# Attention kernel on one Trainium2 core: how the queries reach their stacked layout

## The reference

```python
qh = q.reshape(B, S, 16, 16); kh = k.reshape(B, S, 16, 16)
q1 = einsum('bshd,hed->bshe', qh, wq1); k1 = einsum('bshd,hed->bshe', kh, wk1)   # and q2, k2
s1 = einsum('bshe,bthe->bhst', q1, k1) / 4                                        # and s2
attn = softmax(s1) - gain * softmax(s2)
o = einsum('bhst,bthe->bshe', attn, vp)     # then normed per head, times wo, added to x
```

## Time and profile before

| | |
|---|---|
| median of 3 runs | 1498.9 us (1498.68 to 1508.15) |
| profiled execution | 1502.58 us, its span 1500.8 us |
| first attention | about 27 to 770 us of the span |
| PE busy in the span | 1335.3 us (89%), granted clock 0.963 on average |
| DVE, ACT, POOL busy | 1182.6, 1076.6, 729.9 us |

### The profile page before, as it was taken

How to read it: one execution, slowest core, us unless ns; L and a number is a source line. 1 busy time by engine, 2 the same in 40 slices (tenths; PEclk the granted TensorE clock), 3 DMA queues, 4 the chain that set the end, 5 groups by cost and what they waited for, 6 DMA issues and landing times. The chain is left out here.

```text
span 1500.8 us, 30949 instructions
## 1 busy us (share of the span) xinstructions
PE 1335.3 (89%) x11612; PEld 904.7 (60%) x11612; DVE 1182.6 (79%) x1964; ACT 1076.6 (72%) x1810; POOL 729.9 (49%) x1154
## 2 busy tenths in 40 slices
PE   4799999999999999999978999996899986377686
PEld 3566666666666666666645666665667665133374
DVE  4478888788788788877768999985547999799775
ACT  2377777777777777777747888886455655699996
POOL 2156766757676576676665333421126667521000
PEclk9999999999999999999979999999899889599899
DMA  8655866866676685675310000000544442187399
GB/s 165 114 102 102 154 103 116 140 108 130 114 136 114 123 135 99 111 129 99 89 30 1 1 1 1 1 1 19 185 129 116 128 117 65 39 333 305 130 403 365
DMA packets 126469, 178.31 MB, mean 119 GB/s; under 512 B 47586, under 2 KB 78434, under 8 KB 120162
## 3 DMA queue, kind: packets, MB, share of 16 engines
q1 hardware_dynamic: 126032, 176.32, 49.6%
q10 hardware_dynamic: 288, 0.00, 0.0%
HBM read 82.36 MB, written 41.94 MB: 83 GB/s over the span
## 5 line engine op out<-in xcount | busy, mean ns | idle before, releaser
L735 DVE TENSOR_REDUCE neg_max<-psum 128x8 f32<-128x1024 f32 x256 | 313.2, 1223 | 70.4 <-PE psum L544 65.7
L672 ACT ACTIVATE exp_t<-psum 128x512 f32<-128x512 f32 x512 | 281.6, 597 | 49.3 <-PE psum L557 49.1
L838 POOL TENSOR_TENSOR rs<-rs,minus_half 128x16 f32<-128x16 f32 x64 | 186.3, 2912 | 5.0
L557 PEld LDWEIGHTS psum<-q_stack,k_stack 50*128 50x128 f32 x2048 | 137.5, 192 | 78.5 <-issue 75.2
L557 PE MATMUL psum<-q_stack,k_stack 50*128 50x128 f32 x2048 | 173.6, 290 | 0.8 <-ACT exp_t L672 0.8
L568 PE MATMUL psum<-exp_t,v_pad 128*32 128x256 f32 x2048 | 167.6, 400 | 0.0
L677 ACT ACTIVATE o_t<-psum 128x512 f32<-128x512 f32 x128 | 76.5, 598 | 95.6 <-PE psum L568 95.3
L544 PE MATMUL psum<-k_stack,q_stack 48*128 48x256 f32 x1024 | 136.1, 345 | 6.9 <-DVE neg_max L735 6.4
L943 PE MATMUL psum<-f_w,f_xqt 128*128 128x512 bf16 x512 | 125.1, 387 | 5.1 <-DVE f_hid L1071 5.0
L830 POOL TENSOR_TENSOR sq<-u 128x256 f32<-128x256 f32 x64 | 39.2, 612 | 175.7 <-DVE u L752 174.8
L544 PEld LDWEIGHTS psum<-k_stack,q_stack 48*128 48x128 f32 x1024 | 82.6, 193 | 55.8 <-issue 44.3
(11 more groups left out here) (220 smaller groups left out, 3050.4 us busy)
## 6 DMA issues: line engine op xcount, KB each, us to landing
k_stack<-k_hi SPq DMA_DIRECT2D x256, 128.0 KB, 4.6
g_scratch<-f_gelu SPq DMA_DIRECT2D x24, 1024.0 KB, 3.9
f_gelu<-g_scratch SPq DMA_DIRECT2D x24, 1024.0 KB, 14.9
k_stack<-k_lo SPq DMA_DIRECT2D x128, 128.0 KB, 4.7
ctx_t<-in_ctx_t SPq DMA_DIRECT2D x32, 256.0 KB, 5.3
x_state<-in_x SPq DMA_DIRECT2D x16, 512.0 KB, 6.6
v_in<-in_ctx SPq DMA_DIRECT2D x32, 256.0 KB, 5.7
v_scratch<-v_in SPq DMA_DIRECT2D x32, 256.0 KB, 5.0
```

The lines of the kernel that those rows point to most:

```text
L557: r = e.matmul(psum[:, 2 + j, o:o + P], self.k_st[rows, b // 2 % self.NK, pair // 2 % 2, pair % 2, i, pair // 4, b % 2, :], self.q_st[rows ...
L672: e.activation(self.prob[:, n % 3, j].rearrange("p n w t -> p (n w t)"), psum[:, 2 + j, :], ACT.Exp).then_inc(s["exp"], 1)
L735: e.tensor_reduce(self.negm[:, b % 2, :, :, 2 * u:2 * u + 2].rearrange("p j w n -> p j n w"), psum[:, 0:2, :].rearrange("p j (n w k) -> p ...
L838: e.tensor_tensor(self.rs[:, i], self.rs[:, i], self.expo[:, :], ALU.pow).then_inc(s["pool"], 1)
```

## The change

Queries now go the keys' way, in pairs. POOL writes `xn` of both sequences of a pair, its channels reordered within each half. PE turns them as they are, four transposes for the pair (`turn_queries(p)`, tick 16p-14). ACT copies the high part out of PSUM (`q_high`), DVE the rest (`rest_queries`), and SP stacks them by six transfers of 128 KB into 16 partitions each (`stack_queries(p)`, tick 16p-10). `maxima` waits for them to land. The copies into `q_stack` and the spread buffer are gone. `q_stack` has three slots of a pair instead of four of a sequence, `k_hi` and `k_lo` one buffer instead of two. POOL norms queries two sequences further ahead, so x is loaded two sequences earlier, except the second group of eight, which follows the first queries' transfers. Heads are paired differently, and `wo_t` and the index into `v_pad` are permuted to match. A buffer of the next stage moves, with a wait for the end of the attention.

```diff
-    NQ, NK, NC = 4, KEY_SLOTS, 2
+    NQ, NK, NC = 3, KEY_SLOTS, 2
...
+        def stack_queries(p):
+            k = p % self.NQ
+            w.wait_ge(s["q_lo"], p + 1)
+            w.wait_ge(s["st_pe"], 8 * (p - self.NQ + 1))
+            for j in range(2):
+                for part, src in ((0, self.q_hi), (1, self.q_hi), (2, self.q_lo)):
+                    row = SLOT * j + HD0 * part
+                    e.dma_start(self.q_st[row:row + HD0, k].rearrange("e n h s q -> e n (h s q)").bitcast(F32),
+                                src[SLOT * j:SLOT * j + SLOT].rearrange("p h s q -> p (h s q)").bitcast(F32)
+                                ).then_inc(s["q_st"], 16)
...
+            if u == 6 and b % 2 == 0 and 0 <= b + 2 < NSEQ:
+                stack_queries((b + 2) // 2)
             if u == 6 and b in self.CENTRE_LOAD:
...
-            if u == 7 and b % 8 in (2, 4) and 0 <= b // 8 < 6:
-                load_x(b // 8 + 2, b % 8 // 2 - 1)
-            if tick == -12:
+            if u == 7 and b % 8 in (0, 2) and 0 <= b // 8 < 6:
+                load_x(b // 8 + 2, b % 8 // 2)
+            if tick == -8:
...
-        def turn_queries(b, half):
-            w.wait_ge(s["q_lo"], b + 1)
+        def turn_queries(p):
+            w.wait_ge(s["q_norm"], 2 * p + 2)
             w.wait_ge(sh.s["const_loaded"], 16)
...
+            w.wait_ge(s["k_lo"], 2 * p + 2)
+            for h in range(2):
+                for i in range(2):
+                    r = e.transpose(psum[:, 7, (2 * h + i) * P:(2 * h + i + 1) * P],
+                                    self.xn[:, i, h * P:(h + 1) * P], ident[:, :])
             r.then_inc(s["q_t"], 1)
 
         def maxima(b, u):
             n = 4 * b + u
-            w.wait_ge(s["q_st"], 2 * b + 2)
+            self.q_landed(w, b // 2)
...
-                if u in (2, 4) and 0 <= b + 1 < NSEQ:
-                    turn_queries(b + 1, u // 2 - 1)
+                if u == 2 and b % 2 == 0 and 0 <= b + 2 < NSEQ:
+                    turn_queries((b + 2) // 2)
...
-            if p >= 2:
-                self.k_landed(w, p - 2)
+            if p:
+                self.k_landed(w, p - 1)
...
+        def q_high(p):
+            w.wait_ge(s["q_t"], p + 1)
+            if p:
+                self.q_landed(w, p - 1)
+            e.activation(self.q_hi[:, :, :, :].rearrange("p h s q -> p (h s q)"), psum[:, 7, :], ACT.Copy).then_inc(s["q_hi"], 1)
...
-        def q_stack(b, half):
...
+        def rest_queries(p):
+            flat = lambda z: z[:, :, :, :].rearrange("p h s q -> p (h s q)")
+            w.wait_ge(s["q_hi"], p + 1)
+            e.tensor_tensor(flat(self.q_lo), psum[:, 7, :], flat(self.q_hi).bitcast(F32), ALU.subtract).then_inc(s["q_lo"], 1)
...
-            w.wait_ge(s["q_lo"], b - 1)
-            w.wait_ge(s["q_hi"], b - 1)
-            sh.normed(e, self.xn[:, b % 2], b).then_inc(s["q_norm"], 1)
+            w.wait_ge(s["q_t"], b // 2)
...
-            if 0 <= b + 2 < NSEQ:
-                normed_queries(b + 2)
+            if 0 <= b + 4 < NSEQ:
+                normed_queries(b + 4)
...
+            a0.late_free(w)
```

More of the change, by code:

```diff
@@ L332, in __init__ @@
         self.ctx_t = sb("ctx_t", [P, self.NC, 2, 2, P])
[L333 to L335 removed]
+        self.k_hi = sb("k_hi", [P, 2, 2, 2, P], F32R)
+        self.k_lo = sb("k_lo", [P, 2, 2, 2, P], F32R)
+        self.q_hi = sb("q_hi", [P, 2, 2, P], F32R)
+        self.q_lo = sb("q_lo", [P, 2, 2, P], F32R)
         self.xn = sb("xn", [P, 2, D])
[L338 removed]
+        self.q_st = sb("q_stack", [P, self.NQ, 4, 2, 2, P], F32R)
         self.v_pad = sb("v_pad", [P, 2, 2, NH0, VPAD])
@@ L537, in maxima @@
             n = 4 * b + u
-            w.wait_ge(s["q_st"], 2 * b + 2)
+            self.q_landed(w, b // 2)
             self.k_landed(w, b // 2)
             w.wait_ge(s["max"], n)
-            for pair in (2 * u, 2 * u + 1):
+            for h in range(2):
                 for j in range(2):
-                    rows, o = slice(SLOT * j, SLOT * j + MROW), pair % 2 * D
-                    r = e.matmul(psum[:, j, o:o + D], self.q_st[rows, b % self.NQ, pair, :],
-                                 self.k_st[rows, b // 2 % self.NK, pair // 2 % 2, pair % 2, :, pair // 4, b % 2, :], start=True, stop=True)
+                    rows, o = slice(SLOT * j, SLOT * j + MROW), h * D
+                    r = e.matmul(psum[:, j, o:o + D], self.q_st[rows, b // 2 % self.NQ, u, h, b % 2, :],
+                                 self.k_st[rows, b // 2 % self.NK, u // 2, u % 2, :, h, b % 2, :], start=True, stop=True)
             r.then_inc(s["s_pe"], 1)
@@ L552, in scores_t @@
             w.wait_ge(s["exp"], 2 * n)
-            for pair in (2 * u, 2 * u + 1):
+            for h in range(2):
                 for i in range(2):
                     for j in range(2):
-                        rows, o = slice(SLOT * j, SLOT * j + MROW + 2), (2 * (pair % 2) + i) * P
+                        rows, o = slice(SLOT * j, SLOT * j + MROW + 2), (2 * h + i) * P
                         r = e.matmul(psum[:, 2 + j, o:o + P],
-                                     self.k_st[rows, b // 2 % self.NK, pair // 2 % 2, pair % 2, i, pair // 4, b % 2, :],
-                                     self.q_st[rows, b % self.NQ, pair, :], start=True, stop=True)
+                                     self.k_st[rows, b // 2 % self.NK, u // 2, u % 2, i, h, b % 2, :],
+                                     self.q_st[rows, b // 2 % self.NQ, u, h, b % 2, :], start=True, stop=True)
             r.then_inc(s["st_pe"], 1)
@@ L690, in act @@
                 k_high((b + 3) // 2, u - 6)
-            if u == 0:
-                if 0 <= b + 1 < NSEQ:
-                    q_high(b + 1)
+            if u == 3 and b % 2 == 0 and 0 <= b + 2 < NSEQ:
+                q_high((b + 2) // 2)
             if v in (2, 6) and 0 <= o - 2 < NSEQ:
@@ L797, in dve @@
                 rest_keys((b + 2) // 2, 1)
-            if u == 1 and 0 <= b + 1 < NSEQ:
-                rest_queries(b + 1)
+            if u == 5 and b % 2 == 0 and 0 <= b + 2 < NSEQ:
+                rest_queries((b + 2) // 2)
             if v == 7 and 0 <= o - 4 < NSEQ:
@@ L802, in dve @@
                 sh.moments(w, 1, o - 4)
-            if u in (3, 7) and b == 0:
+            if u in (3, 7) and b in (0, 1):
                 sh.wait_x(w, 1)
[L805 to L808, removed]
+                sh.moments(w, 0, 8 + 2 * b + u // 4)
+            if u == 5 and 12 <= b + 12 < NSEQ:
+                sh.wait_x(w, (b + 12) // 8)
+                sh.moments(w, 0, b + 12)
             ahead(tick)
@@ L866, in centre @@
                             ALU.subtract).then_inc(s["centred"], 1)
-        for b in range(-3, NSEQ + 5):
-            if 8 <= b + 9 < NSEQ and (b + 10) % 8 == 0:
-                sh.finish(w, 0, (b + 9) // 8)
+        for b in range(-4, NSEQ + 5):
+            if 8 <= b + 4 < NSEQ and (b + 4) % 8 == 0:
+                sh.finish(w, 0, (b + 4) // 8)
             if 0 <= b - 5 < NSEQ - 8 and (b - 4) % 8 == 0:
```

57 lines of the change are left out of this document (16 added, 41 removed).

## The result

The changed kernel is **slower**: 1557.6 us, the median of 4 runs (1546.51 to 1570.22), beside 1503.5 for the kernel before in its 4 runs on the same chip. The ratio is 1.0317, with a 95% interval of 1.0204 to 1.043. The forecast was 1483 and its range ended at 1525. Executions over 1.5% above the fastest of their kernel are left out of every ratio and interval, but not of the medians in microseconds, among them one of 2376.2 us in experiment 2 and one of 1639.4 in experiment 3 that nothing here explains. The profiled execution is the longest of the four, 1570.2, some 13 us above the median, so its clock and its waits show the loss a little larger than the median does. Lines behind the queries' code moved: `maxima` is now L559, `scores_t` L572, `back` L600, `keys` L525, the stack transfers L428 (keys) and L439 (queries).

What follows compares the result with a forecast made beforehand. PE's instruction list was taken to bound the first attention. 29 pairs x (21.4 - 22.16) = -22, start +6, together -16: profiled 1502.6 becomes 1486.6, less 3.7 for the median, 1483 us; range 1455 to 1525.

Steps and rivals of the forecast that it cites:

- POOL norms as many tiles, two sequences earlier: On POOL, 67% busy: norming the same number of tiles two sequences earlier was to cost nothing.
- granted clock 1.00 there: Sign expected in the profile after: PE's granted clock at 1.00 in windows of 100 us.
- the clock falls: Rival, chance 0.22: PE's new waits lower its clock, losing up to 5.2 us in one pair of three; 1524 us.
- two-pair sums: Chain of transfers and PE steps over two pairs: 42.45 us, or 43.2 with x; 21.2 or 21.6 a pair.
- The work removed from PE: PE in the first attention: transposes removed save 1.60 us a pair, from 22.16 to 20.56.
- The start: Before the steady pairs: six query transfers ahead in SP's queue add 6 us, between 2 and 12.
- The lateness of the transfers: At the even sequence's first `maxima`: queries land at 24.6 us, needed at 23.3, so 1.3 late; mean pair 21.4.
- The DMA share: Sign expected in the profile after: DMA engines' share 0.9 or more in windows of 100 us.
- The price of a transfer: Each query stack transfer of 128 KB takes 1.00 us, between 0.60 and 1.34; six make 6.0 us a pair.
- One more term: ACT: loses four copies of 0.586 us and gets one, 1.8 us less a pair; beside PE, so nothing gained.
- cheaper: Rival, chance 0.20: stack transfers overlap more or start earlier, PE stays the bound at 20.56 us a pair; 1459 us.
- costlier: Rival, chance 0.16: query stack transfers take 1.34 us each, 22.4 us a pair; 1514 us.

Runs made afterwards that it cites:

- experiment 2: Changed kernel with six useless transposes on PE before the first `maxima` wait of each pair; 1545.7 us, ratio 1.0235 to the kernel before.
- experiment 3: Changed kernel with four query transfers a pair instead of six from the fourth pair on, output not the reference's; 1527.6 us, ratio 1.0106.
- Experiment 7: Kernel before the change, with only the second norm's `finish` moved on POOL into the same step as the first norm's; 1539.0 us, ratio 1.0247.
- experiment 5: Changed kernel with the second norm's `finish` moved two POOL steps later, apart from the first norm's; 1535.4 us, ratio 1.0127.
- experiment 6: Changed kernel with interleaved stacked rows and the second norm's `finish` two POOL steps later; 1475.8 us, ratio 0.9812.
- experiment 4: Changed kernel with each key and query stack transfer writing every third partition of 48, not 16 neighbours; 1514.0 us, ratio 1.0037.
- experiment 1: Changed kernel with twelve useless transposes on PE in each odd sequence, to restore PE's old pair length; 1567.0 us, ratio 1.0383.

## Why the prediction was wrong

Two steps failed, and the runs price each.

**The first** is "POOL norms as many tiles, two sequences earlier ... Cost nothing". It counted tiles and busy share and missed an instruction group that comes once in eight sequences and now shares a step with its twin. The cover named there, four ticks of slack for the transposes, did hold; the one behind the block was `square`, for which DVE, then `x_state`, then PE's `back` wait. Experiment 7 prices it alone at 2.5% (36 us). Taken out of the change it gives 1.0317 - 1.0127 = 1.9% (experiment 5), and with interleaved rows 1.0037 - 0.9812 = 2.3% (experiment 6 against 4).

**The second** is the clock, which the sum of the forecast holds at full speed ("granted clock 1.00 there"): it charges a late transfer with its lateness and nothing more. The lateness itself was right. The sum has 27 x (21.4 - 20.56) = 22.7 us of waits for transfers; the trace has 11.5 for `max_rows`, 6.5 for `q_lo` and 1.8 for the context, 19.8. But four of the nine stretches at 1.2 GHz begin behind the waits for `max_rows`. With POOL's collision out of the way (experiment 5) the kernel is still at +1.3%, where the forecast had -1.1% (1483 / 1498.9): this step is 2.4%, about as much as the first.

**The rival "the clock falls"** had this mechanism, and its frequency, one fall in three pairs, is what the trace counts: nine in 27. It came out short twice. A fall cost 57 to 59 us / 9 = some 6.4 us, not 5.2, since two of them are long ones; 5.0 in experiment 7. And PE's idle time is 37.8 us where it had 1.6 in three pairs, 14 in 27. That its frequency came true is in part luck: five of the nine falls have a cause that it did not know. Its chance, 0.22, was too low for a reason that stands in the prediction: my two-pair sums gave a wait of 1.3 us (2.1 with x) *once in two pairs*, and I then wrote it as "a microsecond or so per pair". The mean is the same, the single wait is not, and the falls follow single waits. Without the collision (experiment 5) the change would have come out at +1.3%, 1518 on the forecast's base, inside the range but near its upper end.

**What held.** The work removed from PE: a pair without waits lasts 20.94 us with PE busy 20.64 of them, against 20.56 forecast; the other 0.30 is a wait of `scores_t` for ACT's `exp_t`, which I had left out. The start: +6.8 against +6. The lateness of the transfers: the twelve pairs of after that no fall touched have a mean of 21.6 (20.94 to 22.26), against 21.4. The DMA share: 0.86 over the 27 pairs, 0.91 to 0.96 in eleven of those twelve, 0.9 forecast. The price of a transfer: by the landings that the trace of the changed kernel keeps, the six of a pair are 0.92 us apart in the mean of 27 pairs, against the 1.00 taken. With 27 x 21.4 = 578 the forecast of the stage was 75 us short of 652.7: 57 to 59 are the clock, 9.1 the waits for `x_state`, 6.8 those for `exp_t`.

**One more term was mis-sized**, with no effect: ACT also lost its two spreading copies a pair (L654, 0.65 us each), so it is busy 446.1 - 373.9 = 72 us less over 27 pairs, 2.7 a pair and not 1.8.

**The rivals with cheaper or costlier transfers** both fell as stated: no pair at full clock of the changed kernel is above 22.3 (costlier had 22.4 as the mean), and only where rows were interleaved do nearly all transfers hide.

**Open.** What decides whether a wait brings a fall is not settled (below). That x ahead of them in the queue makes the maxima's rows late was only shown by moving x. The trace fits it: x was issued at 342.38 and took 8.1 us to land, and the rows issued right behind it, for which PE waits at 350.41, took 7.2, where those issued at 330.55, without x, took 5.6 to 6.1. In the 7 us behind 900 us the granted clock is 0.92, where the kernel before has 0.94 in the same stretch; why was not looked into.

## What to carry to other kernels

When work is moved on a helper engine, list what runs only every so many steps and see which step it lands in; two rare groups in one step make a block that no busy share shows. Price a wait by its single length where the bounding engine has a clock that falls, not by its mean per round, and add the fall's own price. When transfers into few neighbouring partitions are the limit, try to spread their destination: here the same bytes then cost a quarter less of the DMA engines' time and, with POOL's order put right, turned a loss of 1.3% into a gain of 1.9%.

## What the runs showed of the hardware beyond that

In this stream of fp32 matmuls the length of PE's single wait does not by itself decide whether the clock falls. In the changed kernel it held at 2.4 GHz behind waits of 0.66 to 0.98 us, and fell behind every wait of 1.04 and more; in experiment 4 it fell behind all six, 1.33 and more. But elsewhere it fell behind 0.73 (experiment 1, at 299.94, with one of 0.47 right behind it) and 0.90 (experiment 2, at 293.41), has one of 0.99, and of three waits of 1.11 in experiment 7 two were followed by a fall. And it held behind 1.00, 1.01 and 1.02 in experiment 5 (at 675.22, 631.84 and 290.76), behind 1.88 and 1.64 in experiment 3 (at 152.42 and 631.31), and behind 1.98 in experiment 2 (at 353.80). Both are seen between 0.7 and 2.0 us, while all 21 waits of 2.04 us and more between 100 and 700 us, in all the profiles here, were followed by a fall.

A fall does not have one length either: in the changed kernel 10 us behind the wait of 1.04, 14 behind one of 2.55 and 31 behind the one of 3.00; in experiment 5 one of 3 us, behind the wait of 1.44 at 404.64.
